# Adding x1 to the warped context in PSUM by an identity product, in the second stage of a decoder layer

## The chip, the cores and the metric

The kernel runs on one core of a Trainium2 chip. The metric is the device time of one execution in microseconds, as the median of several runs. A core has five engines with queues of their own: TensorE (matrix products and transposes, results in PSUM), VectorE, ScalarE, GpSimd and SyncE, whose queue (SP) issues the transfers between device memory and SBUF here. They are synchronised only by the semaphores that the program sets. PSUM has eight banks, here of 128 x 512 fp32 each.

## What is computed

The layer has three parts, each with a residual and a layer norm. The second is the one that the change touches. Cut to that:

```python
x = _layernorm(x + _L0_attn_ref(x, ...))          # first stage: x1
x = _layernorm(x + _L0_xattn_ref(ctx_1024, x))    # second stage: x2
x = _layernorm(x + _L0_ffn_ref(x, ...))           # third stage: output

def _align_one(small, large):                     # small: 77 x 256 context, large: 256 x 256 (x1)
    D = _pairwise_euclidean(small, large)
    R = _dtw_cost(D)
    i_idx, j_idx, valid = _backtrack(R, 77, 256)
    contrib = small[i_idx] * valid[:, None]
    return jnp.zeros((256, 256)).at[j_idx].add(contrib)
```

For each of 32 batches the dynamic-time-warping path assigns rows of the context to the 256 tokens. The sum over these rows (the warped context) is added to x1, and each token's 256 channels are brought to mean 0 and variance 1.

## The kernel before

All data is fp32. A batch is 256 tokens x 256 channels; it lies in SBUF as [128, 2, 256]: 128 partitions, two token tiles (NT = 2) of C = 256 channels.

The kernel is three blocks, one behind the other, with a barrier between them. In each, every engine has its own program, written by hand as a software pipeline: `pipeline(eng, stages, peel, unroll)` takes a list of (stage, lag) and emits steps; in step i it calls each stage in the order of the list for batch i - lag. The first `peel` steps are straight code, the rest a hardware loop of `unroll` steps a turn, then the tail as straight code. So the order of the work on an engine is the order of the list, and only semaphores tie the engines together. `par`, the batch's parity, picks one of two buffers. A stage without a lag (None) runs in every step; `settle` is one, a drain of VectorE.

The second block first computes the path of every batch on VectorE (from about 210 to 418 us, TensorE has nearly nothing to do), and then a loop over the 32 batches. In that loop, batch b goes through these steps:

- SP: `load` (L601) fetches x1 of the batch into `x1_again`, two buffers; `store` (L605) writes x2 out. List: load lag 0, store lag 3.
- ScalarE: `ramps` (L649) makes a ramp from the path's bounds; VectorE: `masks` (L794) turns it into a 77 x 256 mask.
- TensorE: `warp` (L691) multiplies mask and context rows into a bank of PSUM, two products of 256 columns (one for each token tile). Two banks, in turn.
- VectorE: `add` (L803) adds x1 (one instruction of 128 x 512, PSUM + SBUF) and writes `y2` in SBUF.
- VectorE: `stats` (L807) takes the statistics of `y2`, one instruction a tile, `aggr` (L811) makes mean and variance of them.
- ScalarE: `std` (L654), the square root of the variance. VectorE: `recip` (L816) its reciprocal, `shift` (L819) the product of the negative mean and it.
- ScalarE: `norm` (L663), one instruction a tile, reads `y2` and writes x2 in SBUF.
- TensorE: `turn` (L702), four transposes of x2 into PSUM; VectorE: `chan_stats` (L827), statistics of each channel over the tokens, for the third part's batch norm.

The lists before, with lags:

```python
pipeline(act, [(norm, 4), (ramps, 0), (std, 3)], 6)
pipeline(pe, [(turn, 4), (warp, 1)], 6)
pipeline(dve, [(add, 2), (recip, 3), (settle, None), (masks, 0), (shift, 3), (chan_stats, 5),
               (stats, 2), (settle, None), (aggr, 2)], 8, unroll=4)
```

So within one step VectorE does the add of batch i-2, then the reciprocal of batch i-3 (whose aggregate was the last instruction of the step before), and so on. When the loop is over, VectorE aggregates the channel statistics (L837) and the third block, the long feed-forward part, begins.

Of the kernel before, what the change touches and what calls it, by code (L numbers as in the profile page):

```python
# [15 lines left out]
ALU = mybir.AluOpType  # L16
ACT = mybir.ActivationFunctionType
AX = mybir.AxisListType

P = 128  # L20
# [5 lines left out]
def decoder_layer(nc, x, xT, ctx_rows_d, ctx_cols_d, wqkvT_d, bqkv_d, projT_d, projb_d, gamma_d, beta_d, wq_d,  # L26
                  keysT_d, table_d, out_d):
    NB, S2, C = ctx_rows_d.shape
    T = x.shape[0] // NB
    NT = T // P  # L30
# [15 lines left out]
    with ctx:  # L46
# [3 lines left out]
        def sem(name):  # L50
            return ctx.enter_context(nc.semaphore(name))
# [10 lines left out]
        ident = sb("ident", [P, P])  # L62
# [71 lines left out]
        warp_mm = sem("warp_mm")  # L134
        sum2_done = sem("sum2_done")
        shift2_ready = sem("shift2_ready")
        var2_ready = sem("var2_ready")
        std2_ready = sem("std2_ready")
        x2_ready = sem("x2_ready")
# [46 lines left out]
        def later(b, n):  # L186

            return not (isinstance(b, int) and b < n)

        def pipeline(eng, stages, peel, unroll=2, total=NB):  # L190

            def step(i, par):
                for stage, lag in stages:
                    if lag is None:
                        stage()
                        continue
                    b = i - lag
                    if not isinstance(b, int) or 0 <= b < total:  # L200
                        stage(b, (par + lag) % 2)
            for i in range(peel):
                step(i, i % 2)
            with eng.Fori(0, (total - peel) // unroll) as j:
                for u in range(unroll):
                    step(j * unroll + (peel + u), (peel + u) % 2)
            for i in range(total, total + max(lag or 0 for _, lag in stages)):
                step(i, i % 2)

        def dmas(b, par):  # L210

            return 8 * (b - par) + 16
# [339 lines left out]
        with ExitStack() as st:  # L552
            def sw(name, shape, dt=F32):
                return st.enter_context(nc.sbuf_tensor(name, shape, dt))
# [14 lines left out]
            x1_sb = sw("x1_again", [P, 2, NT, C])  # L569
            y2 = sw("y2", [P, 2, NT, C])  # L570
            st2 = sw("st2", [P, 2, NT, 6])
# [5 lines left out]
            ps_bounds = bank[0][0:RP, 0:2 * NB].rearrange("p (a b) -> p a b", a=2)  # L577
            ps_warp = [bank[1 + i][:, :].rearrange("p (t c) -> p t c", t=NT) for i in range(2)]
            ps_x2T = [bank[3 + i][:, :].rearrange("p (c t) -> p c t", c=CC) for i in range(2)]
# [8 lines left out]
            def _(sp):  # L588
# [9 lines left out]
                def load(b, par):  # L598
                    if later(b, 2):
                        sp.wait_ge(sum2_done, b - 1)  # L600
                    sp.dma_start(x1_sb[:, par], one(x1b, b)).then_inc(x1_in[par], 16)  # L601
# [32 lines left out]
            def _(act):  # L634
# [21 lines left out]

                def norm(b, par):
                    act.wait_ge(shift2_ready, b + 1)
                    if later(b, 2):
                        act.wait_ge(x2_out[par], dmas(b, par) - 16)  # L660
                        act.wait_ge(x2T_mm, b - 1)
                    for t in range(NT):
                        last = act.activation(x2_sb[:, par, t, :], y2[:, par, t, :], ACT.Identity,  # L663
                                              scale=rs2[:, par, t:t + 1], bias=nb2[:, par, t:t + 1])
                    last.then_inc(x2_ready, 1)

                pipeline(act, [(norm, 4), (ramps, 0), (std, 3)], 6)
                act.wait_ge(bnvar_ready, 1)
# [3 lines left out]
            def _(pe):  # L672
# [11 lines left out]

                def warp(b, par):

                    pe.wait_ge(mask_ready, b + 1)
                    if later(b, 2):
                        pe.wait_ge(sum2_done, b - 1)
                    for t in range(NT):  # L690
                        mm = pe.matmul(ps_warp[par][:, t, :], mask[:, par, t * P:(t + 1) * P],  # L691
                                       ctx_rows[:, bass.ds(b, 1), :].rearrange("s a c -> s (a c)"),
                                       start=True, stop=True)
                    mm.then_inc(warp_mm, 1)
# [10 lines left out]
                pe.wait_ge(keymap_done, 1)  # L705
                pipeline(pe, [(turn, 4), (warp, 1)], 6)

            @block.vector
            def _(dve):
# [87 lines left out]

                def add(b, par):
                    dve.wait_ge(warp_mm, b + 1)
                    dve.wait_ge(x1_in[par], dmas(b, par))  # L800
                    if later(b, 2):
                        dve.wait_ge(x2_ready, b - 1)
                    dve.tensor_tensor(y2[:, par], ps_warp[par], x1_sb[:, par], ALU.add).then_inc(sum2_done, 1)  # L803

                def stats(b, par):
                    for t in range(NT):
                        dve.bn_stats(out=st2[:, par, t, :], in_=y2[:, par, t, :])  # L807

# [22 lines left out]
                def settle():  # L831
                    dve.drain()
                pipeline(dve, [(add, 2), (recip, 3), (settle, None), (masks, 0), (shift, 3), (chan_stats, 5),
                               (stats, 2), (settle, None), (aggr, 2)], 8, unroll=4)
                dve.drain()
# [488 lines left out]
```

## Time and profile before

| | us |
|---|---|
| median of 3 runs | 3216.68 |
| lowest and highest run | 3213.38, 3218.46 |
| the profiled execution, in all | 3222.22 |
| its span (first to last instruction) | 3220.3 |
| its mean granted TensorE clock | 0.93 |

Of the page, these are the busy shares of the span in 40 equal slices of 80.5 us, in tenths (9 is 90% or more), and the TensorE clock that was granted, in tenths of full speed:

```profile
PE   7960067699999999999999999999999999999997
PEld 5840045477777777877787778787878777777776
DVE  5667877799989899989898989898999999898965
ACT  4720044222222222222121212121222222222210
PEclk9975556899999999999999999999999999999997
```

PE is TensorE's products, PEld its weight loads (they overlap the products), DVE VectorE, ACT ScalarE. Slices one to three are the first block, three to six the path on VectorE, six and seven the changed loop and the start of the third block. In the other views a row is one instruction or a group of them: its line in the kernel, engine, operation, output<-inputs, how many, how long, and the engine's idle time ahead of it with the releaser, the event that ended that idle time ("issue" where the profile shows none). A granted clock of 1.00 is 2.4 GHz, 0.50 is 1.2 GHz. In timelines the instructions of one line that follow each other are one row, and its time goes from the start of the first to the end of the last.

### The profile page before, as it was taken

The page shows a single profiled execution, that of the slowest core. Times are in us where ns is not written, and L with a number is a line of the kernel's source. Part 1 is how long each engine was busy: PE and PEld are TensorE (multiplying, and loading weights), DVE is VectorE, ACT ScalarE, POOL GpSimd, SP SyncE. Part 2 cuts the span into 40 slices and gives each one's busy share as a digit, 9 for nine tenths or more (in the row PEclk, how much of TensorE's full clock was granted, in tenths as well). Part 3 has the DMA queues.
Part 4 walks back from the last instruction along what each step waited for, and adds up shares of the span by engine and source line. Part 5 has one row for each costly group of instructions (what it writes and reads, how often), then busy time and mean ns, then how long its engine had stood idle before and what let it go on. Part 6 is the DMA issues. An engine that isn't in the chain of part 4 may idle for free. (4 is left out here: it accounts for less than half of the span.)

```text
span 3220.3 us, 81228 instructions
## 1 busy us (share of the span) xinstructions
PE 2869.4 (89%) x30692; PEld 2274.4 (71%) x30692; DVE 2770.1 (86%) x8246; ACT 737.4 (23%) x1302; POOL 599.0 (19%) x604
## 2 busy tenths in 40 slices
PE   7960067699999999999999999999999999999997
PEld 5840045477777777877787778787878777777776
DVE  5667877799989899989898989898999999898965
ACT  4720044222222222222121212121222222222210
POOL 1320000122212121212121212122221222222221
PEclk9975556899999999999999999999999999999997
DMA  5550036000000000000000000000000000000000
GB/s 169 173 143 0 0 115 208 5 5 13 14 6 11 12 12 12 12 12 11 12 12 12 12 12 12 12 12 12 12 12 12 12 12 12 12 11 12 8 8 8
DMA packets 88596, 94.14 MB, mean 29 GB/s; under 512 B 6109, under 2 KB 86910, under 8 KB 88062
## 3 DMA queue, kind: packets, MB, share of 16 engines
q1 hardware_dynamic: 88206, 88.74, 9.0%
q8 instruction: 269, 4.41, 0.6%
q14 instruction: 121, 0.99, 0.1%
HBM read 60.94 MB, written 27.79 MB: 28 GB/s over the span
## 5 line engine op out<-in xcount | busy, mean ns | idle before, releaser
L1009 PE MATMUL bank<-x2T,dnT 128*64 128x256 f32 x8192 | 992.3, 383 | 0.4 <-ACT gelh L1111 0.4
L959 POOL TENSOR_TENSOR hot_lo<-hot_lo,valsT 128x512 f32<-128x512 f32 x512 | 535.4, 1046 | 2441.6 <-DVE hot_lo L1216 2441.6
L1214 DVE TENSOR_TENSOR hot_hi<-iota,valsT 128x1024 f32<-128x1024 f32 x512 | 855.1, 1670 | 52.7 <-issue 36.7
L1032 PE MATMUL bank<-up,gelh 128*128 128x256 f32 x4096 | 895.8, 379 | 3.7 <-DVE gelh L1227 3.7
L1032 PEld LDWEIGHTS bank<-up,gelh 128*128 128x128 f32 x4096 | 779.1, 190 | 136.0 <-issue 28.7
L1009 PEld LDWEIGHTS bank<-x2T,dnT 128*64 128x64 f32 x8192 | 618.2, 138 | 182.2 <-issue 12.5
L1022 PEld LDWEIGHTS bank<-hot_lo,hot_hi 128*64 128x64 f32 x16384 | 584.9, 141 | 170.4 <-issue 134.4
L1022 PE MATMUL bank<-hot_lo,hot_hi 128*64 128x64 f32 x16384 | 595.9, 226 | 71.1 <-issue 39.6
L1111 ACT ACTIVATE gelh<-bank 128x512 f32<-128x512 f32 x512 | 305.7, 597 | 836.8 <-PE bank L1009 836.1
L1227 DVE TENSOR_TENSOR gelh<-bank,gelh 128x512 f32<-128x512 f32 x512 | 347.9, 680 | 83.1 <-PE bank L1022 51.8
L1216 DVE TENSOR_TENSOR hot_lo<-offs,valsT 128x512 f32<-128x512 f32 x512 | 349.7, 683 | 0.0
L987 PE MATMUL bank<-keymap,xnT 128*128 128x512 f32 x512 | 239.9, 612 | 9.4 <-DVE top_i L1164 6.2
L1164 DVE FIND_INDEX8 top_i<-top,bank 128x8 uint32<-128x64 f32 x1024 | 205.0, 227 | 0.0
L1160 DVE MAX8 top<-bank 128x8 f32<-128x64 f32 x1024 | 140.8, 220 | 63.1 <-PE bank L987 63.0
L987 PEld LDWEIGHTS bank<-keymap,xnT 128*128 128x128 f32 x512 | 96.9, 195 | 119.8 <-issue 114.2
L1111 ACT ACT_TABLE_LOAD x62 | 79.5, 1283 | 420.4 <-PE bank L1009 420.4
L682 PE MATMUL bank<-fold,lo_hi 128*80 128x32 f32 x4 | 0.7, 326 | 178.5 <-DVEq L785 178.5
L682 PEld LDWEIGHTS bank<-fold,lo_hi 128*80 128x80 f32 x4 | 0.6, 243 | 178.7 <-DVEq L785 178.7
L1100 ACT ACTIVATE vals<-sel 128x64 f32<-128x64 f32 x64 | 16.4, 257 | 412.7 <-DVE sel L1174 412.3
L1100 ACT ACT_TABLE_LOAD x32 | 41.1, 1283 | 304.2 <-DVE sel L1174 304.1
L1178 DVE FIND_INDEX8 sel_i<-sel,pair 128x8 uint32<-128x64 f32 x512 | 101.0, 223 | 0.0
L1186 DVE TENSOR_TENSOR pick<-half_i,iota 128x512 f32<-128x512 uint32 x128 | 82.8, 689 | 4.8
(145 smaller groups left out, 1964.2 us busy)
## 6 DMA issues: line engine op xcount, KB each, us to landing
x_scratch<-x_sb SPq DMA_DIRECT2D x64, 256.0 KB, 2.2
xT_sb<-in_xT SPq DMA_DIRECT2D x32, 256.0 KB, 2.9
x_sb<-in_x SPq DMA_DIRECT2D x32, 256.0 KB, 2.9
x_again<-x_scratch SPq DMA_DIRECT2D x32, 256.0 KB, 2.7
x_tile<-x_scratch SPq DMA_DIRECT2D x32, 256.0 KB, 3.0
x_res<-x_scratch SPq DMA_DIRECT2D x32, 256.0 KB, 2.9
out_y<-yo SPq DMA_DIRECT2D x32, 256.0 KB, 2.2
gelh<-in_table SPq DMA_DIRECT2D x4, 1024.0 KB, 8.9
```

The costliest lines, as they stand in the source:

```text
L959: pool.tensor_tensor(hot_lo[:, q % BUFS], hot_lo[:, q % BUFS], valsT[:, par, 2, TQ * q:TQ * (q + 1), None].to_broadcast([P, TQ, 2 * CL]), ...
L987: mm = pe.matmul(ps_score[p][:, :], xnT[:, k, a, :], keymap[:, k, p * NH * NK:(p + 1) * NH * NK], start=(k == 0), stop=(k == CC - 1))
L1009: mm = pe.matmul(ps_h[q % 2][rows, c, :], dnT[:, k, 2 * q + c, rows], x2T[:, k, :, :].rearrange("p a t -> p (a t)"), start=(k == 0), stop= ...
L1022: mm = pe.matmul(ps_a[q % 2][rows, t * 2 * CL:(t + 1) * 2 * CL], hot_hi[:, q % BUFS, t, rows], hot_lo[:, q % BUFS, t, :], start=True, stop ...
L1032: mm = pe.matmul(ps_out[:, a, :], gelh[:, par, c, a, :], up[:, c, :], start=(c == 0), stop=(c == CL - 1))
L1111: act.activation(gelh[:, par, 2 * q:2 * q + 2, :, :].rearrange("p c a t -> p c (a t)"), ps_h[q % 2], ACT.Gelu).then_inc(gel_ready, 1)
L1160: dve.max(out=top[:, p, h, :], in_=ps_score[p][:, h * NK:(h + 1) * NK])
L1164: last = dve.max_index(out=top_i[:, p, h, :], in_max=top[:, p, h, :], in_values=ps_score[p][:, h * NK:(h + 1) * NK])
L1178: dve.max_index(out=sel_i[:, h, :], in_max=sel[:, h, :], in_values=pair[:, h, :, :].rearrange("p a b -> p (a b)"))
L1214: dve.tensor_tensor(hot_hi[:, q % BUFS], iota[:, None, 0:P].to_broadcast([P, TQ, P]), valsT[:, par, 0, some, None].to_broadcast([P, TQ, P] ...
L1216: dve.tensor_tensor(hot_lo[:, q % BUFS], offs[:, None, :].to_broadcast([P, TQ, 2 * CL]), valsT[:, par, 1, some, None].to_broadcast([P, TQ, ...
L1227: dve.tensor_tensor(some, ps_a[q % 2][:, :].rearrange("p (t a c) -> p c a t", t=TQ, a=2), some, ALU.mult)\
```

## The change

`y2`, the add and its semaphore `sum2_done` are gone. Behind each of the two products of a warp, TensorE does a second one with the identity matrix as weights and x1 as the moving operand, into the same columns of PSUM (start=False), so that the bank then holds warped context + x1. Its semaphore `warp_mm` now stands for the sum. `stats` on VectorE and `norm` on ScalarE read that bank. As it must live until the norm is done, four banks (1, 2, 5, 6) are used in turn instead of two (1, 2); a stage can name its number of lanes in the list, and the loops of ScalarE and TensorE are unrolled four times, with eight peeled steps instead of six. TensorE waits for the load of x1 and, for a bank, for the norm of four batches ago. The load of x1 waits for the warp of two batches ago instead of its add.

```diff
-            y2 = sw("y2", [P, 2, NT, C])
-            ps_warp = [bank[1 + i][:, :].rearrange("p (t c) -> p t c", t=NT) for i in range(2)]
+            ps_warp = [bank[i][:, :].rearrange("p (t c) -> p t c", t=NT) for i in (1, 2, 5, 6)]
...
                 def load(b, par):
                     if later(b, 2):
-                        sp.wait_ge(sum2_done, b - 1)
+                        sp.wait_ge(warp_mm, b - 1)
...
-                def norm(b, par):
+                def norm(b, lane):
+                    par = lane % 2
                     act.wait_ge(shift2_ready, b + 1)
...
-                        last = act.activation(x2_sb[:, par, t, :], y2[:, par, t, :], ACT.Identity,
+                        last = act.activation(x2_sb[:, par, t, :], ps_warp[lane][:, t, :], ACT.Identity,
...
-                pipeline(act, [(norm, 4), (ramps, 0), (std, 3)], 6)
+                pipeline(act, [(norm, 4, 4), (ramps, 0), (std, 3)], 8, unroll=4)
...
-                def warp(b, par):
-
+                def warp(b, lane):
+
+                    par = lane % 2
                     pe.wait_ge(mask_ready, b + 1)
-                    if later(b, 2):
-                        pe.wait_ge(sum2_done, b - 1)
+                    pe.wait_ge(x1_in[par], dmas(b, par))
+                    if later(b, 4):
+                        pe.wait_ge(x2_ready, b - 3)
                     for t in range(NT):
-                        mm = pe.matmul(ps_warp[par][:, t, :], mask[:, par, t * P:(t + 1) * P],
-                                       ctx_rows[:, bass.ds(b, 1), :].rearrange("s a c -> s (a c)"),
-                                       start=True, stop=True)
+                        pe.matmul(ps_warp[lane][:, t, :], mask[:, par, t * P:(t + 1) * P],
+                                  ctx_rows[:, bass.ds(b, 1), :].rearrange("s a c -> s (a c)"),
+                                  start=True, stop=False)
+                        mm = pe.matmul(ps_warp[lane][:, t, :], ident[:, :], x1_sb[:, par, t, :], start=False, stop=True)
                     mm.then_inc(warp_mm, 1)
...
-                pipeline(pe, [(turn, 4), (warp, 1)], 6)
+                pipeline(pe, [(turn, 4), (warp, 1, 4)], 8, unroll=4)
...
-                def add(b, par):
+                def stats(b, lane):
                     dve.wait_ge(warp_mm, b + 1)
-                    dve.wait_ge(x1_in[par], dmas(b, par))
-                    if later(b, 2):
-                        dve.wait_ge(x2_ready, b - 1)
-                    dve.tensor_tensor(y2[:, par], ps_warp[par], x1_sb[:, par], ALU.add).then_inc(sum2_done, 1)
-
-                def stats(b, par):
                     for t in range(NT):
-                        dve.bn_stats(out=st2[:, par, t, :], in_=y2[:, par, t, :])
+                        dve.bn_stats(out=st2[:, lane % 2, t, :], in_=ps_warp[lane][:, t, :])
...
-                pipeline(dve, [(add, 2), (recip, 3), (settle, None), (masks, 0), (shift, 3), (chan_stats, 5),
-                               (stats, 2), (settle, None), (aggr, 2)], 8, unroll=4)
+                pipeline(dve, [(recip, 3), (settle, None), (masks, 0), (shift, 3), (chan_stats, 5),
+                               (stats, 2, 4), (settle, None), (aggr, 2)], 8, unroll=4)
```

## Rows read from the trace of the kernel before

**Rows 1.** One turn of VectorE's loop by windows: window, length, busy (instructions), clock, DMA.

```profile
454.37:467.76 13.39, 11.26 (x33) 7.66 (x33) 11.42 (x42) 7.13 (x16) 0.00 (x0) 0.50 0.50 156
```

**Rows 2.** VectorE's timeline over that turn: start, duration, engine, line, idle before.

```profile
454.37 0.15 DVE L816 RECIPROCAL rs<-sd 128x2 f32<-128x2 f32 x1
...
456.80 0.25 DVE L811 BATCH_NORM_AGGREGATE mv<-st 128x2 f32<-128x6 f32 x2
457.03 0.69 DVE L803 TENSOR_TENSOR y<-bank,x_again 128x512 f32<-128x512 f32 x1
457.64 0.16 DVE L816 RECIPROCAL rs<-sd 128x2 f32<-128x2 f32 x1
...
466.53 0.25 DVE L811 BATCH_NORM_AGGREGATE mv<-st 128x2 f32<-128x6 f32 x2
467.15 0.69 DVE L803 TENSOR_TENSOR y<-bank,x_again 128x512 f32<-128x512 f32 x1 [0.37 <-issue]
467.76 0.15 DVE L816 RECIPROCAL rs<-sd 128x2 f32<-128x2 f32 x1
```

**Rows 3.** Groups by line, 421 to 530 us: busy us, mean ns, idle before.

```profile
L691 PE MATMUL bank<-ctx_rows,mask 77*128 (+1 forms) x128 | 61.0, 635 | 1.7 <-DVE mask L794 1.7
...
L827 DVE BATCH_NORM_STATS2 bn<-bank 128x256 f32 (+1 forms) x64 | 24.1, 416 | 0.9 <-PE bank L702 0.8
...
L803 DVE TENSOR_TENSOR y<-bank,x_again 128x512 f32<-128x512 f32 x32 | 22.0, 689 | 4.6 <-issue 2.3 <-PE bank L691 1.9 <-ACT x_sb L663 0.3
```

**Rows 4.** VectorE's timeline at the last batch of the loop.

```profile
525.70 0.25 DVE L811 BATCH_NORM_AGGREGATE mv<-st 128x2 f32<-128x6 f32 x2
526.31 0.17 DVE L816 RECIPROCAL rs<-sd 128x2 f32<-128x2 f32 x1 [0.36 <-ACT sd L654]
```

**Rows 5.** Instructions on the tiles y: duration in ns (min/median/max), first and last start.

```profile
L509 DVE BATCH_NORM_STATS2 st<-y x64: 399/414/430, 37.7 to 190.5; 128x6 f32<-128x256 f32 x64
...
L807 DVE BATCH_NORM_STATS2 st<-y x64: 400/405/418, 424.6 to 525.2; 128x6 f32<-128x256 f32 x64
L663 ACT ACTIVATE x_sb<-y,nb,rs x64: 583/593/601, 427.0 to 527.2; 128x256 f32<-128x256 f32 x64
```

**Rows 6.** Groups by line, 440 to 640 us.

```profile
L1085 ACT ACTIVATE xnT<-bank,bn_shift,bn_scale 128x256 f32<-128x256 f32 x4 | 2.0, 559 | 3.3 <-PE bank L978 3.3
```

**Rows 7.** TensorE's timeline in the changed loop, clock 0.50.

```profile
473.47 1.11 PE L702 MATMUL bank<-ident,x_sb 128*128 128x128 f32 x4 [0.61 <-ACT x_sb L663]
474.38 1.91 PE L691 MATMUL bank<-ctx_rows,mask 77*128 x4
```

**Rows 8.** TensorE's timeline in the first stage, clock 1.00.

```profile
61.35 0.60 PE L394 MATMUL bank<-ident,x_sb 128*128 128x128 f32 x4
61.79 1.03 PE L405 MATMUL bank<-x1T,ctxm 128*80 128x256 f32 x4
62.65 0.59 PE L407 MATMUL bank<-x1sum,ones 128*80 128x256 f32 x2
```

**Rows 9.** Windows around rises of the clock; first busy column TensorE, clock third from last.

```profile
34.70:38.00 3.30, 3.30 (x10) 2.57 (x10) 3.16 (x18) 1.55 (x2) 0.00 (x0) 0.50 0.00 0
38.10:51.50 13.40, 9.25 (x49) 6.97 (x47) 12.79 (x54) 5.07 (x14) 1.82 (x2) 1.00 0.34 100
...
421.20:426.70 5.50, 5.46 (x12) 3.69 (x12) 3.48 (x10) 1.31 (x3) 0.00 (x0) 0.50 0.15 48
...
535.70:539.80 4.10, 4.10 (x5) 1.83 (x6) 0.00 (x0) 0.42 (x1) 0.00 (x0) 0.50 1.09 360
539.90:546.00 6.10, 6.10 (x48) 5.25 (x47) 4.34 (x38) 4.09 (x9) 0.00 (x0) 1.00 1.09 349
```

**Rows 10.** DMA issues of the page: engine, count, size, median us to landing.

```profile
x_again<-x_scratch SPq DMA_DIRECT2D x32, 256.0 KB, 2.7
```

**Rows 11.** VectorE's timeline at the start of the loop.

```profile
423.32 0.69 DVE L803 TENSOR_TENSOR y<-bank,x_again 128x512 f32<-128x512 f32 x1 [1.59 <-PE bank L691]
...
426.13 0.16 DVE L816 RECIPROCAL rs<-sd 128x2 f32<-128x2 f32 x1
```

More of the change, by code:

```diff
@@ L134, in decoder_layer @@
         warp_mm = sem("warp_mm")
-        sum2_done = sem("sum2_done")
         shift2_ready = sem("shift2_ready")
@@ L190, in pipeline, with step @@
         def pipeline(eng, stages, peel, unroll=2, total=NB):
-            def step(i, par):
-                for stage, lag in stages:
+            def step(i, lane):
+                for stage, lag, *lanes in stages:
                     if lag is None:
@@ L200, in step @@
                     if not isinstance(b, int) or 0 <= b < total:
-                        stage(b, (par + lag) % 2)
+                        stage(b, (lane - lag) % (lanes[0] if lanes else 2))
             for i in range(peel):
-                step(i, i % 2)
+                step(i, i)
             with eng.Fori(0, (total - peel) // unroll) as j:
                 for u in range(unroll):
-                    step(j * unroll + (peel + u), (peel + u) % 2)
-            for i in range(total, total + max(lag or 0 for _, lag in stages)):
-                step(i, i % 2)
+                    step(j * unroll + (peel + u), peel + u)
+            for i in range(total, total + max(lag or 0 for _, lag, *_ in stages)):
+                step(i, i)
         def dmas(b, par):
```

## The prediction

> **What bounds the kernel now.** I read the slices of the page first: TensorE's clock dips twice, and the code places the changed loop in the second dip, at 421 to 529 us of 3220. So the change touches some 108 us, 3.4% of the span. The third stage, over 2500 us, runs no changed line. A gain or loss of 0.2% of the kernel (6.4 us, about what a measurement of it can tell from no change) is 0.2 us in each of the 32 batches.
>
> Next, one turn of VectorE's loop, four batches, by its window [rows 1]: 13.39 us, TensorE busy 84% at a granted clock of 0.50 (the 1.2 GHz level), VectorE 85%, ScalarE 53%. No engine is full, so the order of events must tell what bounds. VectorE's timeline [rows 2] shows it. A batch goes from the reciprocal at 454.37 to the next at 457.64, 3.27 us: the aggregate starts 2.43 behind the reciprocal, the add 0.23 behind the aggregate, the next reciprocal 0.61 behind the add. At the loop's branch (last three rows) the add starts 0.62 behind the aggregate instead of 0.23. Nothing there waits for another engine. VectorE's program order is the bound, and the add (0.69 us, 32 of them [rows 3]) is part of it.
>
> **The change part by part.**
>
> *The add goes from VectorE.* At first sight that is 32 x 0.69 = 22 us. It isn't, because the add also covers something. A batch ends with aggregate(b), add(b+1), reciprocal(b); between the first and the last, ScalarE takes the square root of b's variance. Without the add the reciprocal stands right behind the aggregate and waits for the root. One place shows this bare, the last batch, which has no add behind its aggregate [rows 4]: aggregate at 525.70 for 0.25, 0.36 idle until the root, reciprocal at 526.31. That is 0.61 us from aggregate to reciprocal, where the loop takes 0.23 + 0.61 = 0.84, and 0.62 + 0.61 = 1.23 at the branch. I take it that the branch and the register work of the next step run while VectorE waits for the root, since the 0.62 from aggregate to add at the branch is as long as that wait. So the new batch is 2.43 + 0.61 = 3.04 us, the turn 12.16.
>
> *The statistics read PSUM.* The same instruction on the same shape takes 416 ns from PSUM [rows 3] and 405 from SBUF in this stage, 399 to 430 in the first [rows 5]. I take +10 ns, two a batch, +0.02; bounds 0 and +30 ns (2 us in all). The turn becomes 12.24, and the gain 13.39 - 12.24 = 1.15 us a turn, 6.9 us over six turns (steps 8 to 31). The Trainium skill (VectorE: DVE Perf Modes, "The TRN2 errata") speaks against this edit: it puts the fixed cost of a VectorE instruction at 58 cycles with an SBUF source and 120 with one in PSUM. By that, as an estimate from the page, each statistic would cost 65 ns more, 4.1 us in all, and the turns would gain only 3 us; the 11 ns between the two rows here do not agree with it.
>
> *The norm reads PSUM on ScalarE.* The nearest rows are 593 ns from SBUF [rows 5] and 559 for the same shape from PSUM in the third stage [rows 6]: 0 to 34 ns less. As the root waits for the aggregate anyway, less brings nothing; I take zero.
>
> *TensorE gets two more products a batch.* A product of 256 fp32 columns is two instructions here. At 1.2 GHz the four of a batch's warp take 1.91 us [rows 7], the last for 0.63 [rows 3], so one adds (1.91 - 0.63)/3 = 0.43; the four transposes take 474.38 - 473.47 = 0.91. So TensorE's work is 0.91 + 4 x 0.43 = 2.63 us a batch now and 0.91 + 8 x 0.43 = 4.33 after. **That is more than VectorE's 3.06**: at 1.2 GHz the change makes TensorE the bound. At 2.4 GHz the first stage gives the price: four transposes 61.79 - 61.35 = 0.44, four 256-column instructions 62.65 - 61.79 = 0.86 [rows 8], so 0.44 + 1.72 = 2.16 us, well under 3.06.
>
> *So the sign hangs on the clock* [rows 9]. It was 0.50 from 34.7 to 38.0 with the engine busy without a gap, and 1.00 behind that; the same from 535.7 to 539.8. It stayed at 1.00 from 38.1 to 51.5 though the engine was busy only 9.25 of 13.4 us (69%), and from 539.9 to 546 on little but transposes. Against it: from 421.2 to 426.7 the engine was busy almost without a gap, and it stayed at 0.50. In today's loop TensorE has a gap ahead of each batch's transposes (0.61 in rows 7) and never rises. After the change, at 1.2 GHz, the gap closes: 4.33 us of work against 3.06 of everything else. The waits don't reopen it: a norm ends about 4 us behind its warp, and its transposes are queued two batches (8.6 us) behind; x1's load, 2.7 us to landing [rows 10], is released two warps ahead. So I expect a dense stretch from 421.2 on, the clock to rise in it and then to stay, as 2.16 of 3.06 us (71%) is about the load that held it from 38.1 to 51.5.
>
> *Start of the stage.* The first add starts at 423.32 [rows 11] behind four instructions; with eight the sum is ready at 425.0, and the first statistics start at about 425.4 where they were at 424.6. The third step's mask waits for the second warp, ready between 427.7 and 428.4, which puts the second reciprocal at about 430.2; now it is at 428.8, 2.7 behind the first at 426.13. That is +1.4. The peeled steps behind it are shorter by 0.1 to 0.6 each. Net +0.3, or +1.7 if the clock rises one batch later; I take +0.5.
>
> *End of the stage.* The peeled steps lose what the add took beyond the root's wait, and the last transposes are shorter by up to 0.47 (0.91 against 0.44): -0.2 to -1.2, I take -0.7.
>
> *Waits that move.* On SP's queue x1's load waits for a warp instead of the later add; the store of x2 behind it comes no later. TensorE now waits for x1 itself, with the next batch's transposes queued behind that wait. At 3.06 us a batch the load is released with the store of x2, some 2.8 us behind a reciprocal, and with 2.7 to land it arrives about when its warp is due. VectorE needs that warp's sum only 1.9 us later; that cover holds the edit at nothing, and without it each microsecond of lateness would cost one. The wait on the norm of four batches ago is satisfied long before.
>
> *The stage behind.* The third stage starts with products at 0.50 (535.7 to 539.8). TensorE has some 4 us without work ahead of them in any case, so I give nothing for a warm start; it would be worth up to 2.2 us.
>
> **Sum.** -6.9 + 0.5 - 0.7 = -7.1 us. The profiled execution has a span of 3220.3 (3222.2 in all), so 3213.2 expected there; it lies 5.5 us above the median of the runs, 3216.7, and against the median the forecast is **3209.6 us**. With the bounds of the terms (turns -4.9 to -6.9, start +0.3 to +1.7, end -0.2 to -1.2, warm start -2.2 to 0) this case alone gives 3206.7 to 3213.3, and with 2 us for the spread of the runs 3204.7 to 3215.3.
>
> **The rivals.**
> *The clock stays low.* For it: the 5.5 busy microseconds from 421.2 that brought no rise, and that the 77-row warp remains half of the products. Against it: both rises in rows 9. Price: 4.33 us a batch, 32 batches 138.6, and about 4.5 from the last warp to the last statistics, against 107.9 now: +35 us, **3252**. It decides as soon as a batch's work on TensorE passes today's 3.35 us, which happens only at 1.2 GHz. This is the slower side.
> *The clock swings.* It rises in dense stretches and falls back in the loop. Half the batches at 4.33 and half at 3.06 would give 118 us plus the tail's 4.5: +15 us, **3231**, less if short falls are hidden by the 1.9 us of slack. The 69% that held the clock speak against. The Trainium skill (TensorE: Matmul & The Clock Gate, "A second HAM failure mode: psum-queue depth-cycling") tells of a kernel whose clock swung as it cycled through PSUM banks; no stretch of this trace shows that.
> *The root's wait takes all.* Root, register work and branch come one after the other: 0.84 from aggregate to reciprocal and 1.23 at the branch, as today: **3216.7**. For it: the root stands behind norm and ramp on ScalarE with under 0.1 us to spare. Against it: rows 4.
> *PSUM reads are dear* while TensorE writes other banks: 30 ns on each statistic, in series on VectorE, is 64 x 0.03 - 0.6 = +1.3 us on the forecast, **3210.9**. By the skill's cycles named above it would be 3213.1.
>
> **How the numbers follow.** Forecast case 0.66, clock low 0.12, clock swings 0.05, root's wait 0.12, PSUM reads 0.05. The forecast case straddles the bound of 0.2% (3210.2): 0.42 below it, 0.24 above. So faster 0.42; same 0.24 + 0.12 + 0.05 and 0.01 of swings that hardly cost, 0.42; slower 0.12 + 0.04 = 0.16. The range takes in all but the clock's rivals, and some of the cheap swings: 3204.5 to 3223.
>
> **What would show it.** Right: 3.06 us from reciprocal to reciprocal with 0.3 to 0.4 idle ahead of each, put down to the root, also at the branch; clock 1.00 from about 428 on; statistics near 416 ns; the last channel statistics at about 522 instead of 529. Wrong: a clock of 0.50 over the stage and TensorE without gaps; or a mask that waits for a warp that waits for x1; or 0.8 and more between aggregate and reciprocal.

## The result, and the profile after

The kernel after takes **3188.2 us** (median of 6 runs, 3185.7 to 3189.9) against 3217.0 before (6 runs on the same chip, 3213.4 to 3218.5): a ratio of 0.9909, 95% interval 0.9899 to 0.9919. It gained 28.8 us where 7.1 were forecast, and the time lies below the range that was given.

First the page of the kernel after, its slices (each now 79.6 us) and the row of its instruction queue.

```profile
DVE  5667867799999999999999999999999999999965
...
PEclk9975589899999999999999999999999999999997
...
q8 instruction: 270, 4.42, 0.6%
```

The reader should look behind the changed stage. From slice 8 on it is the third stage. Before, VectorE's row has 8 and 9 mixed in slices 9 to 38; now it has 9 in all of them. That is a stage in which no line of the kernel changed.

**The second stage** came out as predicted. Groups by line from 415 to 530 us (busy us, mean ns, idle before and its releasers):

```profile
L692 PE MATMUL bank<-ctx_rows,mask 77*128 (+1 forms) x128 | 41.7, 408 | 7.3 <-DMA x_again<-x_scratch 3.6 <-issue 2.8 <-DVE mask L796 0.8
L695 PE MATMUL bank<-x_again,ident 128*128 128x256 f32 x128 | 39.1, 387 | 0.0
L662 ACT ACTIVATE x_sb<-bank,nb,rs 128x256 f32<-128x256 f32 x64 | 32.6, 559 | 34.9 <-DVE nb L815 34.9
...
L803 DVE BATCH_NORM_STATS2 st<-bank 128x6 f32<-128x256 f32 x64 | 23.8, 411 | 0.0
...
L812 DVE RECIPROCAL rs<-sd 128x2 f32<-128x2 f32 x32 | 5.3, 166 | 12.2 <-ACT sd L652 12.2
```

The add of rows 3 is gone, and its place is taken by a wait of the reciprocal for the square root, 12.2 us in 32 batches. VectorE's timeline over two batches of a turn shows it one by one:

```profile
460.09 0.74 DVE L803 BATCH_NORM_STATS2 st<-bank 128x6 f32<-128x256 f32 x2
460.90 0.25 DVE L807 BATCH_NORM_AGGREGATE mv<-st 128x2 f32<-128x6 f32 x2
461.51 0.17 DVE L812 RECIPROCAL rs<-sd 128x2 f32<-128x2 f32 x1 [0.36 <-ACT sd L652]
...
463.96 0.25 DVE L807 BATCH_NORM_AGGREGATE mv<-st 128x2 f32<-128x6 f32 x2
464.58 0.17 DVE L812 RECIPROCAL rs<-sd 128x2 f32<-128x2 f32 x1 [0.36 <-ACT sd L652]
...
467.66 0.17 DVE L812 RECIPROCAL rs<-sd 128x2 f32<-128x2 f32 x1 [0.36 <-ACT sd L652]
```

From reciprocal to reciprocal it is 464.58 - 461.51 = 3.07 us and 467.66 - 464.58 = 3.08, with no extra at the branch, where rows 2 had 3.27 and 0.39 more at the branch. The clock, by windows of the same kernel (first busy column TensorE, clock third from last):

```profile
420.40:424.60 4.20, 4.17 (x10) 3.40 (x11) 0.79 (x2) 1.02 (x2) 0.00 (x0) 0.50 0.00 0
424.60:430.00 5.40, 4.55 (x24) 3.70 (x23) 3.78 (x17) 2.19 (x6) 0.00 (x0) 1.00 0.49 146
455.37:467.66 12.29, 10.07 (x48) 7.32 (x48) 9.21 (x37) 6.84 (x16) 0.00 (x0) 1.00 0.56 171
```

One turn is 12.29 us where rows 1 had 13.39, and TensorE, busy 82% of it with twice the products in its warp, is at 2.4 GHz. The stage is measured from the first product on the finished path (L682 before, L681 after) to the channel aggregate: 418.8 to 530.0 before, 418.0 to 522.4 after. It went from 111.2 us to 104.4: **-6.8 us**.

**The third stage** holds the rest. Its layer norm takes one square root a batch, so the first and the last of the 32 bracket its loop. The row of that instruction (min/median/max ns, first and last start) of before, then of after:

```profile
L1117 ACT ACTIVATE sd<-mv,eps_col x32: 295/296/298, 713.9 to 3216.3; 128x2 f32<-128x2 f32 x32
```

```profile
L1113 ACT ACTIVATE sd<-mv,eps_col x32: 295/295/297, 707.2 to 3181.9; 128x2 f32<-128x2 f32 x32
```

Before, 2502.4 us lie between the two; after, 2474.7: **-27.7 us**. The spans differ by 34.5 us (3220.3 and 3185.8): the first of these square roots comes 6.7 us earlier, and 27.7 us more are gained up to the last. The medians differ by less, since before's profiled execution (3222.2) lies 5.2 us above the median of its six runs and after's does not.

What differs inside the loop shows on TensorE's timeline just behind the loop's branch. Before, its weight loads (start, duration, [idle before]):

```profile
940.96 0.13 PEld L1022 LDWEIGHTS bank<-hot_lo,hot_hi 128*64 128x64 f32 x1 [0.63 <-issue]
943.86 0.95 PEld L1022 LDWEIGHTS bank<-hot_lo,hot_hi 128*64 128x64 f32 x30 [2.77 <-issue]
```

and its products:

```profile
943.86 1.09 PE L1022 MATMUL bank<-hot_lo,hot_hi 128*64 128x64 f32 x31 [3.13 <-issue]
```

After, the products of the same place:

```profile
933.97 1.15 PE L1018 MATMUL bank<-hot_lo,hot_hi 128*64 128x64 f32 x32
934.95 1.03 PE L1005 MATMUL bank<-x2T,dnT 128*64 128x256 f32 x7
936.67 1.24 PE L1005 MATMUL bank<-x2T,dnT 128*64 128x256 f32 x9 [0.70 <-issue]
```

Before, one weight load runs and then TensorE stands for some 3 us with nothing that the profile shows to wait for. After, 39 products with 40 weight loads run first and the stop is 0.70. TensorE's waits between 700 and 3180 us (us in all, times, longest), before and after, by the row that is put down to "issue":

```profile
PE bank L1022 <- issue: 39.6, 13, 3.6
```

```profile
PE bank L1005 <- issue: 10.4, 13, 1.3
```

Thirteen times each, once for each passage through the branch. And before, the stop is sometimes followed by a fall of the clock. Windows of before around the next stop, which ends at 1106.05:

```profile
1100.00:1106.10 6.10, 3.76 (x20) 3.10 (x19) 2.88 (x7) 0.00 (x0) 0.00 (x0) 1.00 0.03 8
1106.10:1108.50 2.40, 2.40 (x38) 2.23 (x39) 0.96 (x3) 0.00 (x0) 1.04 (x1) 0.57 0.02 7
1108.50:1112.00 3.50, 3.50 (x53) 3.10 (x51) 3.33 (x9) 1.31 (x2) 0.00 (x0) 0.80 0.00 0
```

The granted clock was 1.00 up to the stop and mostly 0.50 for 3.4 us behind it, though the engine was then busy without a gap. Eight of the 13 stops in before's loop have such a dip, of 3.4 or 6.8 us; in after there is none before 3080 us, behind the last of its 13 stops.

A loop's branch, a stop for nothing, and a queue of instructions with 270 packets for 4.42 MB (16.4 KB each) suggested a cause: TensorE's instructions are fetched in blocks, and behind a branch it stands until the block is there. The trace of before shows the block itself. Inside the stop, from the weight load at 940.96 to the restart at 943.86, the DMA view (40 slices of 0.0725 us) has one packet of the instruction queue:

```profile
DMA  0000009000000400000000000000000000000000
...
q8 instruction: 1, 0.02, 2.6%
```

It starts in the seventh slice, at 941.4, and 2.6% of 16 engines' 2.9 us make 1.2 us, so it ends at 942.6, and TensorE goes on 1.2 us later. (The second digit is a smaller packet of another queue.) By the packets of the trace it is so at all 13 stops of before: the packet starts 0.2 to 0.9 us behind that weight load, and TensorE goes on 1.2 to 1.6 us behind its end.

In the built programs the head of the third stage's loop stands 176 instructions later in TensorE's program after than before. The change added these 176 instructions, none of them in the third stage. The experiments put that to the test.

### The profile page after: what moved, and what is told of

Its sections match the earlier page's. It is cut to its first block and busy times, and to the rows that moved or that the text cites. A ratio compares the mean times of both kernels' runs of the same rounds, so it can differ in the third digit from the quotient of the medians.

```text
span 3185.8 us, 81364 instructions
## 1 busy us (share of the span) xinstructions
PE 2859.7 (90%) x30820; PEld 2254.4 (71%) x30820; DVE 2753.5 (86%) x8214; ACT 734.6 (23%) x1302; POOL 598.9 (19%) x604
## 3 DMA queue, kind: packets, MB, share of 16 engines
q8 instruction: 270, 4.42, 0.6%
## 5 line engine op out<-in xcount | busy, mean ns | idle before, releaser
L1005 PE MATMUL bank<-x2T,dnT 128*64 128x256 f32 x8192 | 996.8, 381 | 10.8 <-issue 10.4
L681 PE MATMUL bank<-fold,lo_hi 128*80 128x32 f32 x4 | 0.7, 326 | 178.7 <-DVEq L787 178.7
L681 PEld LDWEIGHTS bank<-fold,lo_hi 128*80 128x80 f32 x4 | 0.6, 244 | 178.9 <-DVEq L787 178.9
L1096 ACT ACTIVATE vals<-sel 128x64 f32<-128x64 f32 x64 | 16.4, 257 | 416.3 <-DVE sel L1170 415.9
```

The costliest lines, as they stand in the source:

```text
L1005: mm = pe.matmul(ps_h[q % 2][rows, c, :], dnT[:, k, 2 * q + c, rows], x2T[:, k, :, :].rearrange("p a t -> p (a t)"), start=(k == 0), stop= ...
```

## The experiments

The stall of the loop is given below as TensorE's waits put down to issue between 700 and 3180 us; "the third loop" is first to last of the square roots named above. Increments of a semaphore that nobody waits for serve to move code. They stand in the second block on TensorE, ahead of its wait of some 180 us for the path, so that they cost no time themselves:

```diff
+                for _ in range(N):
+                    pe.sem_inc(pe_rests, 1)
                 pe.wait_ge(path_done, 1)
```

**1. The kernel before, with N = 176**, as many as the change adds.

> The kernel before, with 176 semaphore increments added to TensorE's program in the second block, ahead of its wait for the path (it waits there from about 240 to 418 us anyhow). 176 is the number of instructions by which the change lengthens TensorE's program ahead of the third stage's loop. Theory A (the place of that loop's head in the program sets how long TensorE stands still for instructions behind the loop's branch, 13 times): the stall of 2.3 to 3.6 us at the second product behind the head moves to some 40 products behind it and shrinks to 0.7 to 1.3 us, the dips of the granted clock after it go, and a turn of the third loop takes 161.4 us instead of 163.5. Time about 3217 - 27 = 3190 us or, counting the second stage as unchanged, 3188.2 + 7.6 = 3196 us; I expect 3190 to 3197. Theory B (the third stage is faster because of what the second stage's change leaves behind, such as a warm clock or other PSUM banks): 3217 us, no change.

Measured: 3190.6 us (3188.4 to 3193.3) against 3218.3, ratio 0.9918 [0.9901, 0.9934]. The second stage is the old one with its add, 111.2 us. The third stage's square root:

```profile
L1120 ACT ACTIVATE sd<-mv,eps_col x32: 296/298/299, 713.9 to 3182.6; 128x2 f32<-128x2 f32 x32
```

and TensorE's wait:

```profile
PE bank L1012 <- issue: 12.1, 13, 1.4
```

The third loop takes 2468.7 us, and none of its stops is followed by a dip of the clock. So 27.7 us by the medians are to be had without the change, by 176 instructions that do nothing.

**2. The kernel after, with N = 80**, which puts the head 176 + 80 = 256 instructions behind before's, so that it stands in its block of 256 as before's does.

> The changed kernel with 80 such increments at the same place, which bring the head of TensorE's third loop to the same place modulo 256 instructions (16 KB) as in the kernel before (176 + 80 = 256). Theory A: the third stage is as slow as before, 163.5 us a turn, and only the second stage's 7 to 8 us of gain are left: 3217 - 7.6 = 3209 us, which is what the prediction said. Theory B: 3188 us, as the changed kernel.

Measured: 3214.4 us (10 runs, 3208.4 to 3222.1) against 3218.3, ratio 0.9986 [0.9977, 0.9996]. TensorE's timeline behind the branch, its wait, and the square root:

```profile
1101.44 1.97 PE L1021 MATMUL bank<-hot_lo,hot_hi 128*64 128x64 f32 x32 [2.90 <-issue]
```

```profile
PE bank L1021 <- issue: 38.6, 13, 3.3
```

```profile
L1116 ACT ACTIVATE sd<-mv,eps_col x32: 295/296/298, 708.4 to 3210.9; 128x2 f32<-128x2 f32 x32
```

The timeline row has the old stop, the waits have the old sum, and the third loop is 2502.5 us, before's to 0.1. The second stage kept most of its gain (107.2 us, from 416.3 to 523.5). This is the change as it was forecast: 3.9 us gained by the medians (1.3 to 7.4 by the interval), 5.5 by the spans, against 7.1.

The second stage is 2.8 us longer here than in after, and the trace shows where. Some 0.9 us come at its start, where the clock rose to 1.00 only at 425.3 (9.0 us behind the first product on the path, 6.6 in after). The other 1.9 come at 453 to 457. TensorE waits 1.20 us for x1, at the end of that wait the clock falls to 0.50 for 6.8 us, and VectorE's masks wait for the slower warps, 1.64 us here and 0.94 for the next. First TensorE's timeline, then a window at the low clock (clock third from last), then VectorE's timeline:

```profile
449.32 1.22 PE L695 MATMUL bank<-ctx_rows,mask 77*128 x2 [1.20 <-DMA x_again<-x_scratch]
```

```profile
452.00:456.00 4.00, 4.00 (x13) 3.19 (x12) 2.30 (x9) 1.71 (x4) 0.00 (x0) 0.50 0.36 111
```

```profile
453.24 0.48 DVE L799 SCALAR_TENSOR_TENSOR mask<-iota,bounds,ramp 77x256 f32<-77x256 f32 x1 [1.64 <-PE bank L698]
```

**3. The kernel after, with N = 130.**

> The changed kernel with 130 such increments: some 200 instructions of TensorE now stand between the loop's head and the next multiple of 16 KB instead of some 80. Theory A in full: the 80 covered all but 0.7 to 1.3 us of the stall, 200 cover it whole, a turn takes 160.4 us and the kernel 3188 - 13 x 1.0 = 3175 us. Rival: VectorE's own stall of 2.8 us behind its loop's branch takes over as the bound, and the gain is 0 to 5 us: 3183 to 3188 us. Theory B: 3188 us.

Measured: 3185.6 us, ratio 0.9902 [0.9885, 0.9918]. TensorE's waits:

```profile
PE bank L1021 <- DVE gelh L1226: 21.7, 25, 3.0
...
PE bank L1021 <- issue: 1.2, 5, 0.3
```

The stop is gone, and the time is that of the kernel after (3186.0 in experiment 5, 3188.2 above). The forecast of 13 us more fell, the rival held: once TensorE stops for less than about 1 us, it waits for VectorE instead (19.0 us in after, 21.7 here). The third loop takes 2472.9 us, so the 10.4 us of short stops in after were nearly all hidden. The page's row of the instruction queue gives a second sign that it is a matter of blocks, 12 packets fewer than in after, about one for each of the 13 turns, though the program is longer:

```profile
q8 instruction: 258, 4.23, 0.6%
```

**4. The kernel after, with the mask ahead of the reciprocal**, so that the wait for the square root is covered by an instruction that has nothing to do with it.

```diff
-                pipeline(dve, [(recip, 3), (settle, None), (masks, 0), (shift, 3), (chan_stats, 5),
+                pipeline(dve, [(masks, 0), (recip, 3), (settle, None), (shift, 3), (chan_stats, 5),
```

> The changed kernel with VectorE's list in the order mask, reciprocal, drain, shift instead of reciprocal, drain, mask, shift: independent work stands where VectorE now waits 0.36 us for the square root. If the root's wait and the drain behind the reciprocal are on the bounding chain, as the prediction put it, a batch of the second stage shrinks from 3.09 to about 2.6 us and the kernel gains 12 to 16 us: 3172 to 3176 us. If the load of x1 or TensorE (2.16 us a batch) sets the pace at once, it gains under 5 us: 3183 us or more.

Measured: 3182.0 us (3179.3 to 3184.7), ratio 0.9885 [0.9869, 0.9902]. VectorE's timeline:

```profile
463.39 0.25 DVE L807 BATCH_NORM_AGGREGATE mv<-st 128x2 f32<-128x6 f32 x2
463.72 0.48 DVE L796 SCALAR_TENSOR_TENSOR mask<-iota,bounds,ramp 77x256 f32<-77x256 f32 x1
464.12 0.15 DVE L812 RECIPROCAL rs<-sd 128x2 f32<-128x2 f32 x1
...
466.07 0.25 DVE L807 BATCH_NORM_AGGREGATE mv<-st 128x2 f32<-128x6 f32 x2
```

No idle ahead of the reciprocal is left, and a batch takes 466.07 - 463.39 = 2.68 us instead of 3.07. The second stage is 95.6 us long, 8.8 less than in after. The medians show 4 to 6 us of it (3186.0 and 3188.2 in after, on other chips), less than the 12 to 16 that were expected; the third loop was 5.2 us longer in this profile (2479.9). New limits come up in the stage: the mask waits for the warp that frees its buffer, and TensorE for x1 (waits from 421 to 530 us: in all, times, longest).

```profile
PE bank L692 <- DMA x_again<-x_scratch: 7.9, 13, 0.9
DVE mask L796 <- PE bank L695: 7.9, 11, 3.3
```

**5. The kernel after once more**, beside experiments 6 to 8 on their chip.

> The changed kernel once more, unchanged, as the common reference for the three runs beside it. Both theories: 3188 us; its ratio to the kernel before near 0.991.

Measured: 3186.0 us (3185.1 to 3189.1) against 3221.4, ratio 0.9891 [0.9871, 0.991]. Second stage 104.1 us, third loop 2473.2.

**6. The kernel after, with 26 increments on VectorE** at the start of the third block. VectorE's program is 26 instructions shorter than before's, and these move its loop back to before's place.

```diff
+                for _ in range(26):
+                    dve.sem_inc(dve_pads, 1)
                 dve.tensor_copy(offs[0:64, :], iota[0:64, 0:2 * CL])
```

> The changed kernel with 26 semaphore increments on VectorE at the start of the third block, where it waits some 8 us for the first scores. The change had made VectorE's program 26 instructions shorter, so this brings its third loop back to the place it has in the kernel before. Theory A2 (the 0.3 us a turn by which the changed kernel's third loop, 161.4 us, is longer than that of the shifted kernel before, 161.1, come from the place of VectorE's code): a turn of 161.1 us and 4 to 5 us less than the changed kernel, 3183 to 3184 us. Rival (they come from ScalarE's longer program or are noise between executions): 3188 us.

Measured: 3184.1 us (3182.2 to 3185.7), ratio 0.988 [0.9861, 0.9899]. The third loop takes 2469.5 us, 3.7 less than in experiment 5 and near the 2468.7 of experiment 1, whose VectorE program is before's. But the loop began 3.5 us later (709.7 against 706.2), and the two profiled executions have the same span, 3183.4 us. The medians differ by 1.9 us and the intervals overlap, so a gain from VectorE's place is suggested and not shown. It would explain why experiment 1, without the gain in the second stage, comes so close to the kernel after.

**7. Mask first, and N = 130 on TensorE.**

> The changed kernel with the mask ahead of the reciprocal on VectorE and 130 increments on TensorE in the second block: the two gains together. If they add up, 3182 us less the 2 to 3 us of the shift alone: 3179 us. If VectorE's place in the code is the bound of the third loop, no gain from the shift: 3182 us.

Measured: 3178.8 us (3177.4 to 3180.4), ratio 0.9866 [0.9848, 0.9885]. Second stage 96.1 us, third loop 2475.3.

**8. The same, with 25 increments on VectorE.**

> As the run before, and 25 increments on VectorE at the start of the third block, which put its third loop where the kernel before has it. Theory A2: 4 to 5 us less than the run before, some 3175 us. Rival: no difference, 3179 us.

Measured: **3175.9 us** (3172.5 to 3181.0), ratio 0.9859 [0.9837, 0.9881], the fastest of all: 45 us below before on its chip and 10 below after. Third loop 2469.5 us. Against experiment 7 the medians differ by 2.9 us and the intervals overlap.

The first three experiments show that the place of the code decides, at three places. The last four ask for the rule. In after, 40 weight loads and 39 products run from the loop's head to the stop, in before one weight load. With the few waits between them that puts the end of the block about 82 and about 2 instructions behind the head, and 80 is by how much the heads differ (176 in blocks of 256). The stop ends about as long behind the head in both: 936.67 - 933.97 = 2.70 us in after, 943.86 - 940.96 = 2.90 in before. Over all 13 passages of before it is 2.4 to 3.3 us. So the rule would be: *TensorE can go on 2.4 to 3.3 us behind the head, when the next block is there, and it stops for what the instructions left in its block don't fill.* With N increments on the kernel after, (82 - N) modulo 256 are left. Each of the next four was run once, so their times have no interval; the traces carry the argument.

**9. N = 336**: 256 more than in experiment 2, again 2 left.

> The kernel after with 336 single semaphore increments ahead of the third block on TensorE, 256 more than in the run with 80. Theory (instructions arrive in blocks of 256, 16 KB each, and the place of the loop's head within its block sets the stall): 256 more change nothing, so TensorE's waits put down to issue in the third loop are those of the run with 80, 38 to 40 us in 13 waits at the first products behind the branch, longest 3.3, and the loop from first to last square root takes 2500 to 2505 us. Rival (any shift finds a stall of its own, there is no period): some other sum, anywhere from 0 to 40 us, and a loop of 2470 to 2500.

TensorE's wait:

```profile
PE bank L1021 <- issue: 39.8, 13, 3.4
```

Third loop 2503.6 us (706.4 to 3210.0), 3216.7 in all. The period of 256 holds.

**10. N = 42**: 40 left.

> The kernel after with 42 increments. Theory: the block ends 38 to 40 instructions behind the loop's head, some 20 products with their weight loads, about 0.7 us of work. The next block is there 2.7 to 2.9 us behind the head as in the kernels before and after, so the stall stands within the first 32 products and lasts 2.0 to 2.3 us, 13 times, 26 to 30 us in all; loop 2487 to 2495 us. Rival without a rule for the place: some other sum between 0 and 40 us, or another line.

TensorE's timeline at one passage of the branch, and its wait:

```profile
1097.51 0.79 PE L1021 MATMUL bank<-hot_lo,hot_hi 128*64 128x64 f32 x19 [0.26 <-issue]
1100.43 0.57 PE L1021 MATMUL bank<-hot_lo,hot_hi 128*64 128x64 f32 x13 [2.13 <-issue]
```

```profile
PE bank L1021 <- issue: 28.4, 15, 2.4
```

Nineteen products, then 2.13 us of nothing, and TensorE goes on 1100.43 - 1097.51 = 2.92 us behind the head. Third loop 2489.0 us, 3202.8 in all: both as expected.

**11. N = 107**: 231 left.

> The kernel after with 107 increments, between the run with 80 (stall of 3 us) and the one with 130 (none). Theory: with 80 the head lies 2 instructions ahead of a block's end; 27 more put it some 230 instructions ahead of the next end, more work than the 2.8 us that a block takes, so no stall: under 2 us of issue waits in all, loop 2469 to 2475 us. Rival (the stall falls off smoothly from 80 to 130): about 15 to 25 us in 13 waits, loop 2480 to 2492.

TensorE's wait:

```profile
PE bank L1021 <- issue: 0.2, 1, 0.2
```

No stop; third loop 2474.7 us, 3187.4 in all. As in experiment 3, the page has 258 packets of instructions. From 80 to 107 increments the stall falls from 38.6 us to 0.2, by a step and not by a slope.

**12. N = 198**: 140 left.

> The kernel after with 198 increments. Theory: 140 instructions are left behind the head, 58 more than in the kernel after, whose stall of 0.7 to 1.3 us comes behind 2.0 us of work; the added ones are more than 1 us of work, so no stall, or 13 of under 0.2 us: 0 to 3 us in all, loop 2469 to 2475 us. Rival without a rule for the place: some sum between 3 and 40 us.

No stop either (waits put down to issue: 1.0 us in four); third loop 2476.5 us (1.5 more than expected), 3190.9 in all. The page has 271 packets of instructions; with 2, 40 and 82 left it has 269 to 271. The missing stop also rules out a period of 128, by which 12 would be left here, and a stop of over 2 us due. In a table, by what is left behind the head:

| left in the block | kernel | issue waits, us | third loop, us |
|---|---|---|---|
| 2 | before | 39.6 | 2502.4 |
| 2 | after, N = 80 | 38.6 | 2502.5 |
| 2 | after, N = 336 | 39.8 | 2503.6 |
| 40 | after, N = 42 | 28.4 | 2489.0 |
| 82 | after | 10.8 | 2474.7 |
| 82 | before, N = 176 | 12.7 | 2468.7 |
| 140 | after, N = 198 | 1.0 | 2476.5 |
| 208 | after, N = 130 | 1.2 | 2472.9 |
| 231 | after, N = 107 | 0.2 | 2474.7 |

## Why the prediction was wrong

**The step that failed** is one sentence in the part on the bound: "The third stage, over 2500 us, runs no changed line." It was taken to mean that the third stage costs what it did. But the change adds 176 instructions to TensorE's program ahead of it (four unrolled steps instead of two, more peeled ones, two more products a step), so every instruction behind them lies elsewhere in the blocks of 256 in which the program arrives. The 13 stops behind the loop's branch went from about 3 us to 0.8 on average (0.5 to 1.3). That is 28.8 us less of issue waits, and 6.3 more of waits for VectorE (16.4 to 22.7). The rest of the 27.7 us, some 5, would be the clock that no longer dips behind a stop; that share was not measured apart. Experiments 1 and 2 show it both ways: the gain without the change, and the change without the gain. The stop was in the trace of before, 13 waits of 39.6 us in the longest stage, and I had not asked what ended them, as the change did not touch that stage. No rival had it either.

**The steps on the second stage**, one by one:

- *The add gives back the wait for the root.* Right: 0.36 us idle before the reciprocals of the loop, the number of rows 4, and nothing extra at the branch. Batch 3.06 forecast, 3.07 to 3.08 measured. The rival in which the root's wait takes all fell.
- *Statistics from PSUM.* 411 ns against 405 from SBUF in rows 5, +6 where +10 was taken. The 65 ns more, which the prediction estimated from the Trainium skill's cycles (VectorE: DVE Perf Modes, "The TRN2 errata"), did not come; the rival with dear PSUM reads fell. The prediction's sums had two slips here. With 65 ns on each of eight statistics a turn would gain 13.39 - 12.16 - 0.52 = 0.71 us, six turns 4.3 and not 3. And bounds of 0 and 30 ns give the turns 5.9 to 7.4 us, not 4.9 to 6.9. Neither touches the forecast itself.
- *Norm from PSUM.* 559 ns, the lower bound (rows 6), and as said it brought nothing: ScalarE's norm waits 34.9 us for VectorE.
- *TensorE's two products.* Priced at 0.43 us for one instruction at 1.2 GHz and 0.215 at 2.4. The mean duration in the groups is 387 ns, longer than the latter, as the rows of pipelined products overlap. By the turn's window, TensorE is busy 10.07 us in four batches, 2.5 a batch where 2.16 was worked out: mis-sized by 0.35, still under 3.07.
- *The clock rises in the dense stretch and stays.* Right: 0.50 from 420.4 to 424.6 with TensorE busy 4.17 of 4.20 us, 1.00 behind that and at 82% busy in the loop. It rose at about 424.6, some 3 us before I expected it. Both rivals on the clock fell in after. A swing did come in experiment 2 (6.8 us at 0.50 from 449.2), behind a wait for x1 and not from the four banks, and it cost 1.9 us; such a dip of 3.4 us is also in the trace of experiment 11, at 451.3.
- *Start and end.* The second reciprocal came at 428.65, where before had 428.85 and 430.2 was forecast. But the path was done 0.8 us earlier in this profile; counted from the first product on it, the second reciprocal came 10.6 us in, against 10.0. So it lost 0.6 us where +1.4 was taken for it: with the clock up early the first warps were quicker than forecast. The channel aggregate came at 522.4 instead of 530.0, and 0.8 of these 7.6 us is again the earlier path.
- *x1's load.* TensorE waited 3.6 us for it in 12 waits, 0.5 at most, and VectorE waited for TensorE only at the start (3.6 us in two waits of the first masks) and for 0.6 at the last transposes. The cover of 1.9 us held. In experiment 2 one wait of 1.20 us was covered too, and cost time only by the clock that fell behind it. In experiment 4, with a batch of 2.68 us, the same wait is 7.9 us.
- *The warm start of the third stage* did not come. The clock fell to 0.50 at 520.2 in after, ahead of the third stage, and stayed there for 13.7 us. From the channel aggregate to the third stage's first square root it took 184.8 us, 183.9 before; so zero was fair.

**Where it was right by its mechanism and wrong in the total**: with the third stage put back (experiment 2) the change is worth 3.9 us by the medians and 5.5 by the spans. The second stage was 107.2 us long in that profile and 104.4, 104.1 and 104.9 in the kernels after, after again and with 130 increments; the clock in that one profile, shown above, accounts for the difference. The runs of experiment 2 are spread over 13.7 us (after's over 4.2), and whether the clock does that too, one profile cannot show.

**What stays open.** That VectorE's place matters in the same way rests on 3.7 and 5.8 us of the third loop in two pairs of traces (experiments 5 and 6, 7 and 8) and on medians whose intervals overlap. In both pairs the loop that was shorter also began later, by 3.5 and 2.9 us. VectorE has a stop of its own of some 2.8 us behind its branch, in every kernel (13 times; in after the profile puts five of them down to TensorE), and no place was tried that takes it away. Nor is it shown why some stops of TensorE are followed by a dip of the clock and others of the same length are not: eight of 13 in before, twelve in experiments 2 and 9 with the same stops, seven in experiment 10 with stops of some 2 us, none after the short stops of after and of experiment 1.

## What to carry to other kernels

Before costing the stages behind a change at nothing, look in the trace for stops put down to issue behind the branches of later loops, and count by how many instructions the change moves them: a few added instructions can be worth more than the change. A measured gain of a per cent is then not yet the change's; the kernel before, lengthened by as many idle instructions, is the control that tells the two apart, and a few idle instructions ahead of a hot loop are themselves a cheap thing to tune. And an instruction taken from an engine gives only what is left when the wait that it covered is bare: look for another instruction to cover it, as the mask does in experiment 4.

## What the hardware showed that I had not expected

**Instructions arrive in blocks, and a long loop pays for it at its branch.** The period is 256 instructions (experiments 2 and 9), a packet of the instruction queue 16.4 KB, so 64 bytes an instruction. Behind the branch of a loop that takes 17 such packets a turn (217 from 780 to 2870 us in before, 12.8 turns), TensorE gets at the block after the first 2.4 to 3.3 us behind the loop's head, whatever is left in the first: 2 instructions (stop of about 3 us), 40 (some 2), 82 (0.5 to 1.4), 140 or more (none). That block's packet starts only 0.2 to 0.9 us behind the head in before, as if it were asked for only there. With 208 or 231 left, the program takes 258 packets instead of 269 to 271, about one less a turn. The worst and the best place differ by 30 us in this kernel, 0.9%. The Trainium skill (Runtime: NRT & Kernel Launch, "Instruction fetch mechanics") says that instructions come in blocks of 256 and that a taken branch whose target isn't held on the engine has to fetch it first; the runs agree with both. It calls the cost of passing from block to block mostly hidden; here TensorE's only stops put down to issue from 700 to 3180 us in before are the 13 behind the branch.

**A stop of 3 us can cost twice.** In before the granted clock fell to 0.50 at eight of the 13 stops, for 3.4 or 6.8 us, with TensorE busy without a gap once the stop was over; 31 products took 1.56 us behind the stop that ends at 1106.05 and 1.09 behind the one that ends at 943.86.

**VectorE's statistics hardly mind PSUM**, 411 ns against 405. The Trainium skill (VectorE: DVE Perf Modes, "The TRN2 errata") puts 62 cycles between the two sources; this instruction on 128 x 256 fp32 does not show them.
